# Layer 1's slot in another order on four engines: the output projection at its end beside the attention product, keys and values behind the transposed queries

## What is computed

```python
# layer 1, latents = layernorm(x): 32 query heads, 8 key/value heads, head size 128
kv = concatenate([context, latents], axis=1)           # 256 rows per batch
q = rms_norm(latents @ Wq, q_norm_w)
k = rms_norm(kv @ Wk, k_norm_w);  v = kv @ Wv
scores = einsum(q, k) / sqrt(128)                      # 4 query heads share one key head
out = softmax(scores) @ v                              # per head
x = x + tanh(g_xattn[1]) * (out @ Wo)
x = x + tanh(g_ffn[1]) * (layernorm(x) @ W.T + bias)   # the layer's feed-forward
```

## Time and profile before

| | |
|---|---|
| median of 3 runs | 1681.61 us |
| the profiled execution | 1681.52 us, its span 1679.7 us |
| TensorE busy (matmul) | 1663.4 us, 99% of the span |
| VectorE / ScalarE / GpSimd busy | 1190.1 (71%) / 1001.6 (60%) / 603.5 us (36%) |
| granted TensorE clock | 1.000, mean over the span |
| layer 1's 64 slots | from about 932 us to 1650 us |

### The profile page before, as it was taken

The page is one execution under the profiler, slowest core; times in us unless marked ns, Lnnn a source line. Parts: engine busy times, 40 slices in busy tenths (PEclk is TensorE's granted clock), DMA queues, the critical chain, the costliest instruction groups (busy, mean ns, idle before and its releaser), DMA issues.

```text
span 1679.7 us, 30969 instructions
## 1 busy us (share of the span) xinstructions
PE 1663.4 (99%) x10269; PEld 1477.9 (88%) x10269; DVE 1190.1 (71%) x2245; ACT 1001.6 (60%) x2540; POOL 603.5 (36%) x584
## 2 busy tenths in 40 slices
PE   9999999999999999999999999999999999999998
PEld 8899999999888888888888888888888888888887
DVE  6444446576787787777788877777676767677677
ACT  5344434345767777776776666656666665666563
POOL 2422223201434443534435543333333333333343
PEclk9999999999999999999999999999999999999999
DMA  6444444544233333333332110101010111111001
GB/s 227 175 167 157 150 150 150 192 165 161 95 106 102 112 112 99 126 100 120 108 113 83 39 51 24 63 26 59 12 62 25 52 32 50 36 36 41 14 7 51
DMA packets 80591, 153.31 MB, mean 91 GB/s; under 512 B 6544, under 2 KB 58128, under 8 KB 76944
## 3 DMA queue, kind: packets, MB, share of 16 engines
q1 hardware_dynamic: 80528, 152.50, 26.9%
HBM read 108.43 MB, written 44.04 MB: 91 GB/s over the span
## 4 chain that ended last, share of the span: by engine, by line
PE 87%; DVE 5%; ACT 3%; issue 3%; POOL 2%; DMA 1%; SPq 0%; ACTq 0%; POOLq 0%; DVEq 0%
PE bank L2103 20%; PE bank L2050 15%; PE bank L2052 15%; PE bank L2051 15%; PE bank L2280 7%; PE bank L2500 3%; PE bank L2238 3%; PE bank L2316 3%; PE bank L2400 2%; PE bank L2526 2%; PE bank L2226 1%; DMA vraw<-wv 1%; PE bank L2531 1%; ACT pr L1048 1%; PE bank L2072 0%
## 5 line engine op out<-in xcount | busy, mean ns | idle before, releaser
L2050 PE MATMUL bank<-w_hi,xt_hi 128*128 (+2 forms) x512 | 178.0, 348 | 1.2 <-DVE qt_lo L1949 1.1
L747 POOL TENSOR_TENSOR p<-p,rn 128x512 f32<-128x512 f32 x128 | 133.5, 1044 | 122.1 <-DVE rn L1917 118.8
L2052 PE MATMUL bank<-w_hi,xt_lo 128*128 (+2 forms) x512 | 172.7, 337 | 0.0
L2051 PE MATMUL bank<-w_lo,xt_hi 128*128 (+2 forms) x512 | 171.4, 335 | 0.0
L690 POOL TENSOR_TENSOR pr<-pr,rn 128x512 f32<-128x512 f32 x64 | 67.5, 1055 | 284.3 <-DVE rn L1564 284.3
L1203 ACT ACTIVATE p<-bank,nb,q_r 128x256 f32<-128x256 f32 x256 | 141.2, 562 | 3.3 <-DVE nb L1913 0.8
L609 POOL TENSOR_TENSOR q_r<-q_ms,half 128x4 f32<-128x4 f32 x64 | 64.4, 1007 | 190.6 <-DVE q_ms L1892 190.6
L1048 ACT ACTIVATE pr<-sc,nmax 128x128 f32<-128x128 f32 x256 | 99.9, 391 | 41.6 <-DVE nmax L1549 41.3
L609 POOL TENSOR_TENSOR k_r<-k_ms,half 128x2 f32<-128x2 f32 x64 | 59.3, 927 | 144.3 <-DVE k_ms L1871 144.3
L2050 PE MATMUL bank<-w_hi,ot_hi 128*128 (+1 forms) x256 | 106.2, 415 | 1.3 <-DVE ot_lo L1937 1.3
L2050 PEld LDWEIGHTS bank<-w_hi,xt_hi 128*128 128x128 f32 x512 | 96.2, 188 | 12.4 <-DVE qt_lo L1949 1.6
(11 more groups left out here) (293 smaller groups left out, 5605.2 us busy)
## 6 DMA issues: line engine op xcount, KB each, us to landing
stage<-w SPq DMA_DIRECT2D x35, 512.0 KB, 3.2
keys_of_layer<-kout SPq DMA_DIRECT2D x16, 1024.0 KB, 4.5
values_of_layer<-vout SPq DMA_DIRECT2D x16, 1024.0 KB, 5.2
kt<-keys_of_layer SPq DMA_DIRECT2D x64, 256.0 KB, 3.3
vs<-values_of_layer SPq DMA_DIRECT2D x64, 256.0 KB, 2.8
vraw<-wv SPq DMA_DIRECT2D x10, 1024.0 KB, 6.7
kraw<-wk SPq DMA_DIRECT2D x16, 512.0 KB, 5.6
stage0o<-w SPq DMA_DIRECT2D x16, 512.0 KB, 3.3
```

Source lines behind the costliest of these rows:

```text
L747: pool.tensor_tensor(p1[:, half_p:half_p + 2, :], p1[:, half_p:half_p + 2, :], rn1[:, half_p:half_p + 2].unsqueeze(2).to_broadcast([P, 2, ...
L2050: nc.tensor.matmul(out_ap, l_hi, r_hi, start=(c == 0), stop=False)
L2051: nc.tensor.matmul(out_ap, l_hi, r_lo, start=False, stop=False)
L2052: op = nc.tensor.matmul(out_ap, l_lo, r_hi, start=False, stop=(c == n - 1))
```

## The change

No instruction is added or dropped. Within layer 1's slot the order changes on four engines.

- TensorE: transposed queries of i+1, keys and values of i+2, transposed keys of i+1, probabilities of i, queries of i+2, scores of i+1, output projection of i-1, attention product of i.
- ScalarE: `qt_hi`, then `ot_hi` of unit i-1, `kt_hi`, `kv_out`, `pt_hi`, `q_out`, and at the end the exponentials of unit i+1, which stood at the head of slot i+1.
- VectorE: `qt_lo`, `ot_lo` of unit i-1, `kt_lo`, (`split_lo`), v and k means, `pt_lo`, scaled keys, maxima of i+1, (`split_hi`, and for t = 0 `split_lo`), mean of q, reciprocals of i+1, `accumulate1` of i-1, and `row_stats` in the last group behind it.
- GpSimd: the two roots of unit i+2 and then the multiplication of unit i+1, which stood in front of the next slot's roots.

The first two slots are written out as functions of their own, and the last slot has no keys, values and queries left to make. The diff, cut to the orders:

```diff
@@ GpSimd
-                if not (first and j == 0):
-                    for half_p, done in ((0, norm1_first), (2, norm1_second)):
-                        pool.wait_ge(recip1_done, 2 * i - 1 + half_p // 2)
...
-                if not tail and not (last and j == BODY - 1):
+                ahead = not (last and j == BODY - 1)
+                if ahead:
                     k_root(i + 2)
                     q_root(i + 2, (j + 1) % 2)
+                normalised(i + 1)
@@ ScalarE
+            def second_slot1():
+                queries_hi(2)
+                keys_hi(2)
+                exponentials1(1, 0)
+                transposed_hi(2, 6)
+                transposed_hi(2, 7)
+                kv_out(3, 2, 2)
+                probabilities_hi(1)
+                q_out(3)
+                exponentials1(2, 1)
+                output1_hi(1)
...
+                queries_hi(i + 1)
+                if not (first and j == 2):
+                    output1_hi(i - 1)
+                keys_hi(i + 1)
+                if ahead:
                     wait(act, o1_ps, i - 2)
                     kv_out(i + 2, (j + 1) % 4, 4 * t + (j + 1) // 2 + 1)
+                probabilities_hi(i)
+                if not ahead:
                     transposed_hi(3, 0)
+                if ahead:
                     q_out(i + 2)
+                exponentials1(i + 1, j % 2)
@@ VectorE
+                maxima1(2, 1)
+                output1_lo(1)
+                inverse_sums1(2)
+                split_lo(1, 0, 1)
...
+                queries_lo(i + 1)
+                if not (first and j == 2):
+                    output1_lo(i - 1)
+                keys_lo(i + 1)
                 if first and 2 <= j < 6:
                     split_hi(1, j - 1, 1)
                 if not last and not first and 1 <= j < 6:
                     split_lo(t + 1, j - 1, (t + 1) % 2)
...
                 if ahead:
                     v_low(i + 2, (j + 1) % 4)
                     k_mean(i + 2)
+                probabilities_lo(i)
+                if ahead:
+                    k_scaled(i + 2, (j + 1) % 4)
+                else:
+                    transposed_lo(3, 0)
+                maxima1(i + 1, j % 2)
                 if first and 2 <= j < 6:
                     split_lo(1, j - 1, 1)
                 if not last and not first and j < 5:
                     wait(dve, y1_ps if j >= 3 else q1_ps, 8 * t)
                     split_hi(t + 1, j, (t + 1) % 2)
                 if ahead:
                     q_mean(i + 2)
+                inverse_sums1(i + 1)
+                accumulate1(i - 1, (j - 2) % B)
+                if last and j in (3, 5, 7):
+                    dve.wait_ge(acc1_done, i - 1)
+                    row_stats(3, (j - 3) // 2)
@@ TensorE
+                transposed_queries(i + 1)
                 if ahead:
+                    next_keys_values(t, j, own, other)
+                transposed_keys(i + 1)
                 if first and j == 2:
                     pe.wait_ge(first_lo, 5)
                     pe.wait_ge(xt_lo_done, 3 * B)
+                    output_projection1(1, 0)
+                transposed_probabilities1(i)
+                if not ahead:
                     pe.wait_ge(kt1_lo_done, U)
                     transpose_rows(3, 0)
+                if ahead:
+                    queries((j + 1) % B, other if j == BODY - 1 else own, i + 2)
+                scores1(i + 1)
+                if not (first and j == 2):
+                    output_projection1(i - 1, own if j >= 2 else other)
+                attention_output1(i, (j - 1) % 4)
```

More of the change, by code:

```diff
@@ L1965, in slot1 @@
                     split_lo(t + 1, j - 1, (t + 1) % 2)
-                if not (first and j < 2):
-                    accumulate1(i - 1, (j - 2) % B)
-                if last and j == BODY - 1:
-                    probabilities_lo(i)
-                    transposed_lo(3, 0)
-                if last and j in (3, 5, 7):
-                    dve.wait_ge(acc1_done, i - 1)
-                    row_stats(3, (j - 3) // 2)
                 if last and j == 2:
@@ L2508, in attention_output1, with next_keys_values, transposed_queries, transposed_keys @@
                 op.then_inc(o1_ps, 1)
+            def next_keys_values(t, j, own, other):
+                if j == BODY - 1:
+                    for piece in range(5):
+                        pe.wait_ge(w1_lo_done[piece], t + 1)
+                if isinstance(t, int) and t == 0:
+                    pe.wait_ge(xt_lo_done, 2 * B + j + 2 if j < BODY - 1 else 3 * B)
+                keys_values((j + 1) % B, other if j == BODY - 1 else own, BODY * t + j + 2)
+            def transposed_queries(count):
+                pe.wait_ge(q1_copied, count)
+                pe.wait_ge(q1_squared, count)
+                for a in range(4):
+                    op = nc.tensor.transpose(by4(Q1B[:, :])[:, a, :], by4(q_sb[:, :])[:, a, :], ident[:, :])
+                op.then_inc(qt1_ps, 1)
+            def transposed_keys(count):
+                pe.wait_ge(k1_scaled, count)
+                pe.wait_ge(v1_lo_done, count)
+                for a in range(2):
+                    op = nc.tensor.transpose(KVB[:, tok(a)], k_sb[:, a, :], ident[:, :])
+                op.then_inc(kt1_ps, 1)
+            def scores1(count):
+                pe.wait_ge(qt1_lo_done, count)
+                pe.wait_ge(kt1_lo_done, count)
+                wait(pe, exp1_done, count - 1)
+                for a in range(4):
+                    op = passes(by2((S0B, S1B)[a // 2][:, :])[:, a % 2, :],
+                                [(qt_hi[:, tok(a)], qt_lo[:, tok(a)], kt_hi[:, :], kt_lo[:, :])])
+                op.then_inc(s1_ps, 1)
+            def first_slot1():
+                next_keys_values(0, 0, 0, 1)
+                transposed_queries(1)
+                transposed_keys(1)
+                transpose_rows(2, 4)
+                transpose_rows(2, 5)
+                queries(1, 0, 2)
+                pe.wait_ge(facc_done, B)
+                scores1(1)
+            def second_slot1():
+                next_keys_values(0, 1, 0, 1)
+                transposed_queries(2)
+                transposed_keys(2)
+                transpose_rows(2, 6)
+                transpose_rows(2, 7)
+                queries(2, 0, 3)
+                pe.wait_ge(xt_lo_done, 3 * B - 2)
+                transposed_probabilities1(1)
+                scores1(2)
+                pe.wait_ge(xt_lo_done, 3 * B - 1)
+                attention_output1(1, 0)
             def slot1(t, j):
```

184 lines of the change are left out of this document (76 added, 108 removed).

## The result

| | before | changed |
|---|---|---|
| median | 1681.68 us (8 runs, 1681.17 to 1682.81) | 1687.57 us (8 runs, 1685.35 to 1689.61) |
| ratio | | 1.0034, 95% interval 1.0025 to 1.0043 |
| profiled execution | 1681.52 us | 1689.61 us, span 1687.7 us |

The change costs 5.9 us. The forecast was 1688.4, within 1684.6 to 1692.5. The median hit is luck in good part: as the last sections show, one of the sum's terms was 2.3 us too small, two were 1.7 and 3.3 too large, and a cost that the sum doesn't have filled the rest. The executions of the changed kernel lie 4.3 us apart, those of before 1.6 in this comparison and up to 3.3 in those beside the experiments.

The account below looks back on a forecast made before the run. The prediction took the loop to be bound by TensorE's matmul stream; 2.9 (border) + 1.4 (slots 2 to 5) + 2.5 (last group) = 6.8 on 1681.52 gave 1688.3, forecast as 1688.4 us by the median, range 1684.6 to 1692.5.

Parts of the forecast that it names:

- border of slots 1 and 2: First group: TensorE waits 2.6 us for `ot_lo` of unit 1, then 0.3 more for `p`; 2.9 us in sum.
- slots 2 to 5 of the first group: Whole `w_lo` between maxima and `q_ss` makes `p` late; 0.35 us missing in four slots, 1.4 us.
- last group: Layer 1's end: new waits of 0.5, 0.8, 0.65, 0.9 and 1.1, less 1.5 for removed ones; 2.5 us.
- loop: Layer 1's slots, t = 1 to 6: gains and loses nothing, 0 us.
- The 0.3 for `p` behind it: Slot 2: `p` starts only when `w_lo` ends and comes too late for TensorE; 0.3 us with the semaphore.
- the paragraph on T: T ends a slot's scores; transposes of the probabilities start at T+6.2 again, since the same pieces lie between.
- Its slack: Loop: second half of `p` is done 0.2 us before needed in 30 slots, 0.8 in the other 18.
- so the stream changes by 0.01 us in a slot: TensorE's matmul stream in the loop: new neighbours change it by at most 0.6 us in 62 slots; taken as 0.
- rival C: Not slower: 256-column keys behind transposes swallow the restart, 5.6 us come back, 1682.8 remains; chance 6%.
- The five waits: Last group: `qt_lo` 0.5 and 0.8 (slots 4, 6), `p` 0.65 and `kt_lo` 0.9 (slot 7), `ot_lo` 1.1 (unit 63).
- The 0.8 for slot 6: Last group: statistics' last instruction waits for GpSimd's bias sum until T+7.0, delaying slot 6's queries by 0.8 us.
- Rival B: Waits swallow each other; only slot 2's and two or three small ones remain, 4 us, 1685.5; chance 21%.

Follow-up runs that it names:

- experiment 6: Changed kernel with TensorE's transposed queries between output projection and attention product from slot 3 on; 1687.39 us, ratio 1.0035.
- experiment 7: Changed kernel with 19 added TensorE matmuls, results unused, filling the two long waits ahead of slot 2's projection and slot 3's probabilities; 1686.1 us, ratio 1.0026.
- experiment 1: Changed kernel with slot 1's old end: `ot_hi` of unit 1 ahead of unit 2's exponentials, weights' piece 0 split ahead of its reciprocals; 1683.5 us, ratio 1.0011.
- Experiment 2: Changed kernel with the weights' lo part in slots 2 to 5 of the first group made behind the means of k, as before; 1684.57 us, ratio 1.0020.
- experiment 8: Kernel of experiment 1 with unit 1's output projection moved behind the scores of unit 3; 1683.93 us, ratio 1.0015.
- experiment 5: Kernel before the change with one move: ScalarE makes `ot_hi` of unit 1 behind the exponentials of unit 2; 1685.31 us, ratio 1.0022.
- experiment 9: Changed kernel with slot 1's old end, `w_lo` back in place, last slot's `kt` ahead of `ot` and last `ot_lo` ahead of statistics; 1679.59 us, ratio 0.9990.

## Why the prediction came out

Term by term, as predicted and as measured (at full clock, from start to start of the matmuls):

| step | predicted | measured |
|---|---|---|
| border of slots 1 and 2 | 2.9 | 2.7 |
| slots 2 to 5 of the first group | 1.4 | 3.7 |
| last group | 2.5 | 0.8 |
| loop | 0 | -3.3 |
| clock behind the waits | not in the sum | 2.0 (the remainder) |
| sum | 6.8 | 5.9 |

The two profiled executions close the sum. Their spans, 1687.7 and 1679.7, lie 8.0 apart: 3.9 by the first four terms, 3.0 by the clock (1.4 behind the first wait, 1.6 behind the second), and 1.1 by which the changed kernel's execution begins layer 1 later (940.80 against 939.70). That 1.1 isn't the change's: layer 0 is the same code, and the profiled executions of the experiments begin layer 1 anywhere up to 2.8 us ahead of this one.

**The border** was right in its wait: 2.48 by the row. The two traces whose clock stayed up there, those of experiments 6 and 7, have 14.99 and 14.94 us from the scores of unit 2 to those of unit 3, 2.7 more than before. The row shows less than the slot loses, since it counts from where the profile ends the matmul before, 0.24 us after the next one could have started (0.16 inside a run of transposes). The 0.3 for `p` behind it did not come. `p` took 3.00 us (958.25 to 961.25) beside `w_lo`, as forecast, but no row of TensorE waits for it, not even in experiments 6 and 7. So the total of 2.9 is close because one small term stood for another.

**Slots 2 to 5** is the step that failed. It took the paragraph on T for all slots: "In the new order the same pieces lie there, so these start at T+6.2 again." In slot 2 they don't. The diff has `if not (first and j == 2)` in front of the projection behind the scores, so between the scores of unit 3 and the probabilities of unit 3 there are 3.4 us of work, not 6.2. The waits are 2.56 by the rows, 3.0 from start to start, and the slot costs as much: 11.45 (experiment 1) less 11.23 plus the projection's 2.75, which isn't in it. Slots 3 to 5 cost 0.67 together where 1.05 was forecast. Experiment 2 shows that 1.13 of the 2.28 is `w_lo` in the chain, experiment 8 that the rest belongs to the missing projection and not to its place.

**The loop.** Its slack was right. `p` ends at 1234.56 in a slot with `w_hi`; the fifth transpose starts at 1234.88, 0.32 later (in the 30 slots 0.17 to 0.33, in the other 18 about 1.0; where TensorE waits for `p`, it starts 0.05 behind its end):

```profile
1232.52 2.04 POOL L743 TENSOR_TENSOR p<-p,rn 128x512 f32<-128x512 f32 x2
...
1234.44 1.04 PE L2546 MATMUL bank<-ident,p 128*128 128x128 f32 x8
```

What failed is "so the stream changes by 0.01 us in a slot". The penalty behind transposes is what it said, 0.088 for 256 columns (0.203 less 0.115) and 0.087 for 512 (0.317 less 0.230); rival C, that the small matmuls swallow it, is false by these 0.088, though the loop does give time back, as it alone said. The 0.053 us come from steps that I took as fixed. By block, as means over 35 slots:
- The attention product takes 1.365 instead of 1.386. The first five or six steps of 512 columns behind the scores are 0.228 to 0.236, later ones 0.227. Before, the product stood at such a place; now it follows the projection and has 0.227 in all but its last. The projection has the slower steps in both orders. In experiment 6, where it stands behind transposes, its steps are 0.225 to 0.233 again.
- The projection takes 2.748 instead of 2.841, and the keys 1.478 instead of 1.418; the first is the penalty lost. The second is less than the penalty won, since the keys' twelve matmuls take 1.50 in one slot and 1.45 in the next; before they took 1.418 in each. The scores (+0.010) and the queries (-0.008) cancel.

Why every second slot has the quicker keys is open, and with it about half of the 0.053: without it the keys would take 0.03 more in the mean. Experiment 6 has it too (1.417 and 1.364), with its keys behind the same neighbour as before the change, so that neighbour isn't the reason.

**The last group.** The five waits stand where they were forecast. By the rows they are 0.10 and 0.27 for `qt_lo`, 0.27 for `p`, 0.82 for `kt_lo` and 0.78 for `ot_lo`. The forecast counted from start to start, and so counted they are 0.34 and 0.51 (forecast 0.5 and 0.8), 0.43 (0.65), 1.07 (0.9) and 1.03 (1.1): 3.4 in place of 3.95. The larger error is in the old waits that go. In the same count the three for `ot_lo` were worth 2.0 and not 1.5, and one of 0.3 for `pt_lo`, which the forecast didn't have, went with them. 3.4 less 2.3 is 1.1; the two traces as wholes, from the scores of unit 57 on, give 0.8. The 0.8 for slot 6 rested on the `nb` row, a small instruction held until a bias sum ended. That came too, somewhat earlier: the bias sums begin at 1638.30, and the statistics' last instruction takes 0.34 and ends with the first of them, at T+6.8 (T is 1632.77) instead of T+7.0:

```profile
1638.30 2.51 POOL L631 TENSOR_TENSOR residual<-residual,plain 128x512 f32<-128x512 f32 x2
...
1639.27 0.34 DVE L1326 TENSOR_SCALAR ve<-mv 128x2 f32<-128x2 f32 x1
```

Rival B, that the waits swallow each other, had a last group as small as this, but not by what it names: all five are there.

**The clock.** No step had it. Behind each of the two long waits it may fall to 0.50 for some 3 us, which costs 1.4 to 1.6. Experiments 1, 5 and 7 show it from three sides. It doesn't fall in every execution: experiment 6's trace has it behind its wait of 2.3 us and not behind that of 2.6. The other four terms make 3.9; experiment 7, which pays them and no clock, lies 4.5 above the kernel before. The Trainium skill (TensorE: Matmul & The Clock Gate, HAM oscillation — how this bites in real kernels) tells of a kernel whose TensorE waits for data between its bursts, is throttled each time and begins the next burst at the low level. The traces agree in kind, not in size: the waits in the page's example are of some 3 to 5 us and bring a fall each time; here waits of 1.94 to 2.5 us were enough, in some executions. The same page's Part 1 (What's actually happening) says of the rise to the high level that its moment varies from run to run; that a fall can come in one execution and stay out in another is what these runs show. Why it does is open.

## What to carry to other kernels

When an order is changed in a loop, walk through the first and last passes by themselves: a distance worked out in the loop is false wherever the written-out code leaves a piece out, and one block put later leaves a hole of its own length at the crossing. Price a wait of TensorE of about 2 us or more at its length and up to 1.6 us more here, and look at the granted clock behind it; with 1.15 us as the longest wait of the crossing (experiment 9) the clock never fell. When two executions are compared, look first at where the untouched part ends: here it alone made up to 2.8 us. And don't take a stream's steps as fixed when blocks change neighbours: 0.05 us in a slot, over 62 slots, were worth more than the largest wait.

## What the runs showed of the hardware that was not expected

- Useless work can pay: with 19 matmuls in two waits the clock stayed at 1.000 in nine of nine executions instead of one of eight. The median was 1.5 us lower (with overlapping intervals), and the range 1.2 us instead of 4.3.
- A wait of 1.94 us was enough for the clock to fall to 0.50 behind it (experiment 8).
- The same waits of 2.28 and 0.28 us cost 1.58 us more in one execution than in another, by the granted clock alone.
- A matmul of 512 columns has steps of 0.228 to 0.236 just behind matmuls of 256, and 0.227 once some six of its kind are through; the same keys take 1.50 and 1.45 us in alternate slots. Both are unexplained.
